# A two-layer recurrent block on one core: another order for the first batch's loads, up projections and attention chain

## What is computed

```python
xn = _layernorm(x, axis=-1)
s = _L0_attn_ref(xn, W_qkv, W_o)      # 16 heads of 16, ALiBi bias, causal softmax
g = _silu(_L0_ffn_ref(xn, W1, W2, W3))
x = x + s * g
xn = _layernorm(x, axis=-1)
s = _L1_attn_ref(...)                 # 16 heads of 128, RMS norm, rotation, soft cap, causal
g = _silu(_L1_ffn_ref(...))           # 16 routed experts, top 4, and a shared one
x = x + s * g
# inside _L0_ffn_ref, H = 1024:
hidden = jax.nn.silu(x @ W1.T) * (x @ W3.T)
out = fwht(hidden) @ W2.T             # Walsh-Hadamard transform along H
```

## Time and profile before

| | us |
|---|---|
| median of 3 runs | 1249.67 |
| lowest, highest | 1247.97, 1250.04 |
| the profiled execution, its own time | 1248.96 |
| its span | 1247.2 |

### The profile page before, as it was taken

How to read it: one execution, slowest core, us unless ns; L and a number is a source line. 1 busy time by engine, 2 the same in 40 slices (tenths; PEclk the granted TensorE clock), 3 DMA queues, 4 the chain that set the end, 5 groups by cost and what they waited for, 6 DMA issues and landing times.

```text
span 1247.2 us, 26623 instructions
## 1 busy us (share of the span) xinstructions
PE 1195.5 (96%) x9930; PEld 1048.9 (84%) x9930; DVE 845.9 (68%) x1691; ACT 601.9 (48%) x1353; POOL 498.9 (40%) x489
## 2 busy tenths in 40 slices
PE   4999999999988999999999999999999999999997
PEld 3788888888877777777789999999999999999996
DVE  3656777777677334434478888887887767777686
ACT  3444434444433455555545455554555455556443
POOL 0322334434444100000076776677664534454442
PEclk8999999999999999999999999999999999999999
DMA  6645335524739333333221111011010100000001
GB/s 205 249 162 178 109 115 204 190 74 162 241 133 374 95 107 103 105 106 103 79 91 38 50 33 60 26 65 31 26 60 1 35 1 1 1 1 1 1 27 43
DMA packets 65918, 114.93 MB, mean 92 GB/s; under 512 B 7937, under 2 KB 36481, under 8 KB 64385
## 3 DMA queue, kind: packets, MB, share of 16 engines
q1 hardware_dynamic: 59648, 96.45, 22.9%
q0 software_dynamic: 6144, 16.79, 4.1%
HBM read 48.85 MB, written 60.16 MB: 87 GB/s over the span
## 4 chain that ended last, share of the span: by engine, by line
PE 82%; DVE 6%; issue 5%; POOL 2%; ACT 2%; DMA 1%; SPq 1%; POOLq 0%; ACTq 0%; DVEq 0%
PE bank L837 8%; PE six L854 6%; PE bank L916 5%; PE bank L914 5%; PE bank L915 5%; PE six L955 5%; PE bank L992 2%; PE bank L990 2%; PE bank L991 2%; PE bank L927 2%; PE bank L926 2%; PE bank L928 2%; PE six L956 2%; PE bank L464 2%; PE six L979 2%
## 5 line engine op out<-in xcount | busy, mean ns | idle before, releaser
L1834 DVE TENSOR_TENSOR sq<-xs 128x512 f32<-128x512 f32 x128 | 131.1, 1024 | 39.3 <-ACT xs L1336 39.3
L2056 POOL TENSOR_TENSOR rstd<-msq,half_pow 128x8 f32<-128x8 f32 x64 | 105.9, 1655 | 96.0 <-DVE msq L1841 94.0
L1317 ACT ACTIVATE pT<-six,rstd 128x256 f32<-128x256 f32 x128 | 60.8, 475 | 169.0 <-PE six L956 169.0
L2068 POOL TENSOR_TENSOR pT<-pT,tri_mul 128x512 f32<-128x512 f32 x64 | 81.9, 1279 | 142.8 <-ACT pT L1365 142.8
L1981 POOL TENSOR_TENSOR hid_l<-hid,hid_h 128x256 fp32r<-128x256 f32 x64 | 50.4, 788 | 160.1 <-ACT hid_h L1092 160.0
L837 PE MATMUL bank<-experts,xT 128*128 x316 | 109.8, 470 | 0.8 <-ACT xT L1261 0.8
L914 PE MATMUL bank<-bw_h,xT1h 128*128 128x512 f32 x256 | 105.6, 413 | 0.8 <-ACT v L1341 0.8
L1405 DVE TENSOR_TENSOR yT1l<-six,yT1h 128x512 fp32r<-128x512 f32 x64 | 44.3, 692 | 84.7 <-ACT yT1h L1370 84.7
L916 PE MATMUL bank<-bw_l,xT1h 128*128 128x512 f32 x256 | 100.3, 392 | 0.0
L915 PE MATMUL bank<-bw_h,xT1l 128*128 128x512 f32 x256 | 99.9, 390 | 0.0
L2059 POOL TENSOR_TENSOR qn<-xs,rstd 128x256 f32<-128x256 f32 x128 | 91.4, 735 | 5.0
(11 more groups left out here) (315 smaller groups left out, 3820.8 us busy)
## 6 DMA issues: line engine op xcount, KB each, us to landing
cells_scratch<-zeros SPq DMA_DIRECT2D x8, 4352.0 KB, 16.5
xg<-cells_scratch SPq DMA_DIRECT2D x79, 128.0 KB, 2.0
cells_scratch<-y SPq DMA_DIRECT2D x79, 128.0 KB, 1.7
experts<-pack_experts_dram SPq DMA_DIRECT2D x16, 608.0 KB, 10.5
raw<-pack_attn_dram SPq DMA_DIRECT2D x8, 1024.0 KB, 5.0
qkA<-qkc SPq DMA_DIRECT2D x64, 64.0 KB, 2.4
w_full<-pack_w_dram SPq DMA_DIRECT2D x2, 1024.0 KB, 7.0
out_dram<-x_all SPq DMA_DIRECT2D x8, 256.0 KB, 2.1
```

Of the source, the lines that this page charges most:

```text
L1834: dve.tensor_tensor(out=sq[:, tt, :], in0=x_qk, in1=x_qk, op=ALU.mult).then_inc(sq_sb, 1)
L2056: pool.tensor_tensor(out=rstd[:, r, :], in0=msq[:, r, :], in1=half_pow[:], op=ALU.pow).then_inc(rstd_sb, 1)
```

## The change

Loads. w1 and w3 are loaded in halves: both first halves go ahead of stairs and k_rows, both second halves (`load_ffn(1)`) between the two spreads of the queries and keys. vo moves ahead of them all. The small constants, the gate bias and w2 move from behind the spreads to ahead of them. One semaphore for each half, `ffn_loaded[n]`, replaces `w1_loaded` and `w3_loaded`; the constants now count on `w2_loaded` with w2, so that POOL and `later_consts` wait for all five.

ACT and DVE, before the first batch: vo and the first half of w1 are converted ahead of `query_key`, the first half of w3 ahead of `values`. The second half of w1 is converted after the first `gate_tanh`, that of w3 after the first `heads_T`.

First batch. `up(0, 0)` and `up(0, 1)` come ahead of `scores(0, 0)`; `up(0, 2)` and `up(0, 3)` inside the first group's chain; the four `hadamard_mix` are placed one behind each of the blocks from `scores_T(0, 0)` to `mix(0, 1)`; `up(0, 4)` goes ahead of `scores(0, 3)`; `down(0, 4)` ahead of `scores(1, 0)`. ACT and DVE follow, with `later_consts` now ahead of the first `maxima`. What is computed stays the same, and so does the number of operations but for one load DMA in each of w1 and w3.

```diff
--- before.py
+++ after.py
...
@@ -313,10 +314,20 @@
             sp.dma_start(ident[:], ident_c).then_inc(ident_loaded, 16)
             sp.dma_start(q_row[:], q_row_c).then_inc(ident_loaded, 16)
             sp.dma_start(wqk_full[:].rearrange("p k c -> p (k c)"), pack_qk).then_inc(qk_loaded, 16)
+            sp.dma_start(wvo_full[:], pack_vo).then_inc(vo_loaded, 16)
+
+            def load_ffn(n):
+                for full, pack in ((w1_full, pack_w1), (w3_full, pack_w3)):
+                    sp.dma_start(ffn_half(full, n), ffn_half(pack.rearrange("p (k c) -> p k c", k=KD), n))\
+                      .then_inc(ffn_loaded[n], 16)
+
+            load_ffn(0)
             sp.dma_start(stairs32, stairs_c).then_inc(consts_loaded, 16)
             sp.dma_start(kA.rearrange("p g t -> p (g t)"), k_rows_c).then_inc(consts_loaded, 16)
-            sp.dma_start(wvo_full[:], pack_vo).then_inc(vo_loaded, 16)
-            sp.dma_start(w1_full[:].rearrange("p k c -> p (k c)"), pack_w1).then_inc(w1_loaded, 16)
+            for dst, src in ((hadamard, hadamard_c), (tri_mul, tri_mul_c), (before, before_c)):
+                sp.dma_start(dst[:], src).then_inc(w2_loaded, 16)
+            sp.dma_start(gate_bias[:], gate_b.partition_broadcast(P)).then_inc(w2_loaded, 16)
+            sp.dma_start(w2_a[:], pack_w2).then_inc(w2_loaded, 16)
 
             def spread(b, u):
 
@@ -330,12 +341,8 @@
             sp.wait_ge(consts_made, 1)
             sp.wait_ge(consts_loaded, 16 * N_CONST)
             spread(0, 0)
+            load_ffn(1)
             spread(0, 1)
-            for dst, src in ((hadamard, hadamard_c), (tri_mul, tri_mul_c), (before, before_c)):
-                sp.dma_start(dst[:], src).then_inc(w3_loaded, 16)
-            sp.dma_start(gate_bias[:], gate_b.partition_broadcast(P)).then_inc(w3_loaded, 16)
-            sp.dma_start(w3_full[:].rearrange("p k c -> p (k c)"), pack_w3).then_inc(w3_loaded, 16)
-            sp.dma_start(w2_a[:], pack_w2).then_inc(w2_loaded, 16)
             sp.dma_start(xs_all[:, TT:NT // 2, :],
                          x[1:NB // 2].rearrange("b (t p) d -> p (b t) d", p=P)).then_inc(x_loaded, 16)
             sp.dma_start(route_sb[:], route_c).then_inc(later_loaded, 16)
@@ -656,33 +663,37 @@
                 last.then_inc(fw_done, 1)
 
             def first_batch():
+                pe.wait_ge(wa_lo, 5)
+                pe.wait_ge(v0_sb, 1)
+                up(0, 0)
+                up(0, 1)
                 pe.wait_ge(consts_made, 2)
                 scores(0, 0)
+                pe.wait_ge(hid_sb, 1)
+                up(0, 2)
                 maxima_T(0, 0)
+                pe.wait_ge(hid_sb, 3)
+                up(0, 3)
                 scores_T(0, 0)
+                pe.wait_ge(hid_sb, 2)
+                pe.wait_ge(fw_lo, 1)
+                hadamard_mix(0)
                 scores(0, 1)
                 mix(0, 0, 0)
-                pe.wait_ge(wa_lo, 6)
-                up(0, 0)
+                hadamard_mix(1)
                 heads_back(0, 0)
                 maxima_T(0, 1)
-                up(0, 1)
                 scores_T(0, 1)
-                pe.wait_ge(hid_sb, 1)
-                up(0, 2)
+                hadamard_mix(2)
                 scores(0, 2)
                 mix(0, 1, 0)
-                pe.wait_ge(fw_lo, 1)
-                hadamard_mix(0)
-                pe.wait_ge(hid_sb, 2)
+                hadamard_mix(3)
                 heads_back(0, 1)
                 maxima_T(0, 2)
-                hadamard_mix(1)
                 scores_T(0, 2)
-                hadamard_mix(2)
-                hadamard_mix(3)
-                pe.wait_ge(hid_sb, 3)
-                up(0, 3)
+                pe.wait_ge(wa_lo, 7)
+                pe.wait_ge(hid_sb, 4)
+                up(0, 4)
                 pe.wait_ge(w2_lo, 4)
                 norm_T0(1)
                 down(0, 0)
@@ -692,25 +703,22 @@
                 project(1, 0)
                 heads_back(0, 2)
                 maxima_T(0, 3)
-                pe.wait_ge(hid_sb, 4)
-                pe.wait_ge(wa_lo, 7)
-                up(0, 4)
+                down(0, 1)
+                pe.wait_ge(hid_sb, 5)
+                up(0, 5)
                 scores_T(0, 3)
                 pe.wait_ge(qk_sb, 3)
                 project(1, 1)
-                down(0, 1)
-                pe.wait_ge(hid_sb, 5)
-                up(0, 5)
                 down(0, 2)
+                mix(0, 3, 0)
                 pe.wait_ge(qk_sb, 4)
                 up(0, 6)
-                mix(0, 3, 0)
+                heads_back(0, 3)
                 down(0, 3)
-                heads_back(0, 3)
                 pe.wait_ge(hid_sb, 6)
                 up(0, 7)
+                down(0, 4)
                 scores(1, 0)
-                down(0, 4)
                 down(0, 5)
 
             def batch(b, par, final):
@@ -1116,8 +1124,8 @@
                 o = bank[:, 0:TT * P].rearrange("p (t e) -> p t e", t=TT)
                 act.activation(r_th[:], o[:, :, 0:NE], ACT.Tanh, scale=0.5).then_inc(rth_sb, 1)
 
-            def ffn_hi(loaded, count, w, full, n):
-                act.wait_ge(loaded, 16 * count)
+            def ffn_hi(w, full, n):
+                act.wait_ge(ffn_loaded[n], 32)
                 act.activation(ffn_half(w, n), ffn_half(full, n), ACT.Copy).then_inc(wa_hi, 1)
 
             def hadamard_hi():
@@ -1137,37 +1145,37 @@
                                ACT.Copy).then_inc(v0_sb, 1)
 
             def first_batch():
-                ffn_hi(w3_loaded, N_W3, w3_h, w3_full, 0)
-                exps(0, 0)
-                ffn_hi(w3_loaded, N_W3, w3_h, w3_full, 1)
-                heads_T(0, 0)
                 gate_tanh(0, 0)
-                hadamard_hi()
                 gate_tanh(0, 1)
                 hidden_hi(0, 0)
-                exps(0, 1)
+                ffn_hi(w1_h, w1_full, 1)
                 hidden_hi(0, 1)
                 gate_tanh(0, 2)
+                hadamard_hi()
+                hidden_hi(0, 2)
+                gate_tanh(0, 3)
+                exps(0, 0)
+                hidden_hi(0, 3)
+                down_hi(0)
+                heads_T(0, 0)
+                ffn_hi(w3_h, w3_full, 1)
+                down_hi(1)
+                exps(0, 1)
+                down_hi(2)
                 heads_T(0, 1)
-                hidden_hi(0, 2)
-                down_hi(0)
+                down_hi(3)
                 exps(0, 2)
-                down_hi(1)
-                down_hi(2)
-                down_hi(3)
-                gate_tanh(0, 3)
+                gate_tanh(0, 4)
                 norm_T0(1)
-                hidden_hi(0, 3)
                 heads_T(0, 2)
                 query_key(1, 0)
-                gate_tanh(0, 4)
+                hidden_hi(0, 4)
+                gate_tanh(0, 5)
                 exps(0, 3)
                 query_key(1, 1)
-                hidden_hi(0, 4)
-                gate_tanh(0, 5)
+                hidden_hi(0, 5)
+                heads_T(0, 3)
                 gate_tanh(0, 6)
-                heads_T(0, 3)
-                hidden_hi(0, 5)
                 hidden_hi(0, 6)
                 gate_tanh(0, 7)
 
@@ -1218,12 +1226,12 @@
             qk_hi(0)
             qk_hi(1)
             norm_T0(0)
+            vo_hi()
+            ffn_hi(w1_h, w1_full, 0)
             query_key(0, 0)
             query_key(0, 1)
-            vo_hi()
+            ffn_hi(w3_h, w3_full, 0)
             values(0, 0)
-            ffn_hi(w1_loaded, 1, w1_h, w1_full, 0)
-            ffn_hi(w1_loaded, 1, w1_h, w1_full, 1)
             first_batch()
             for w in range(0, NB // 2 - 1):
...
@@ -1605,34 +1613,33 @@
                 dve.tensor_scalar(out=gate_bias[:], in0=gate_bias[:], scalar1=0.5, scalar2=None, op0=ALU.add)
 
             def first_batch():
+                hidden(0, 0)
+                hidden(0, 1)
+                later_consts()
                 maxima(0, 0)
+                hidden(0, 2)
                 queries_max(0, 0)
-                ffn_lo(5, w1_l, w1_full, w1_h, 1)
-                ffn_lo(6, w3_l, w3_full, w3_h, 0)
-                later_consts()
+                hadamard_lo()
+                hidden(0, 3)
+                ffn_lo(6, w1_l, w1_full, w1_h, 1)
+                down_lo(0)
                 maxima(0, 1)
+                heads_out(0, 0)
+                queries_max(0, 1)
+                stats(1, st0, mv0, ve0, st0_sb, mv0_sb, ve0_sb)
                 ffn_lo(7, w3_l, w3_full, w3_h, 1)
-                queries_max(0, 1)
-                hidden(0, 0)
-                heads_out(0, 0)
-                hadamard_lo()
-                hidden(0, 1)
-                hidden(0, 2)
-                maxima(0, 2)
-                queries_max(0, 2)
-                heads_out(0, 1)
-                stats(1, st0, mv0, ve0, st0_sb, mv0_sb, ve0_sb)
-                down_lo(0)
                 down_lo(1)
                 normalise(1, xn0[:, 1, :, :], mv0, rs0, rs0_sb, xn0_sb)
                 down_lo(2)
+                maxima(0, 2)
```

(23 more changed lines are left out.)

## The result

| | median us | runs | lowest, highest |
|---|---|---|---|
| before | 1249.17 | 7 | 1247.41, 1250.04 |
| changed | 1243.83 | 7 | 1242.80, 1246.90 |

The ratio is 0.9966, 95% interval 0.9956 to 0.9976: faster, by 3.0 to 5.5 us (the quotient of the two medians, 0.9957, is near the upper end of that gain). The profiled execution took 1243.83 us, its span is 1242.0 against 1247.2 us, 5.2 us less. I had forecast 8.8 us and 1240.2. The direction held, and the time lies in the wide range of 1237 to 1246. But it is outside the forecast's own range of 1238 to 1242, and the gain is only 0.6 of what the sum gave.

What follows compares the result with a forecast made beforehand. PE, 82% of the chain of waits, was taken to bound the kernel. Gains of 9.6 us less 0.8 at the batch's end gave 8.8, so 1248.96 became 1240.2; own range 1238 to 1242 (55%), eight in ten 1237 to 1246.

Steps and rivals of the forecast that it cites:

- What bounds the kernel, and what an early microsecond is worth: Whole execution: PE is 82% of the chain of waits; a microsecond saved early is one at the end while PE stays full.
- handed back at the end of the batch: Rival: batch 1's spread, cell clearing or loads hold to absolute times; remaining gain 2 to 3 us, 1246 to 1247; chance 5%.
- Start of `values`: Before the first batch: vo converted early, so values waits only for the second query_key and starts at 15.6 us.
- First up projection: Start of up(0,0): waits for w3's first half converted, w3_l from 17.9 to 19.1, so it starts at 19.1 us.
- The collision with POOL: DVE's w3_l waits behind POOL's first sum over w2, 15.5 to 17.9; up(0,0) starts at 19.1, without it 17.9.
- The second halves: Second-half loads of w1 and w3 in the first batch: landing 24.7 to 27.1 us, ACT's wait costing up to 3, taken as 0.
- queues in the way: Rival: POOL runs both sums first (2.3 us), second halves land late (up to 3), or both; 1242.5 to 1245.5; chance 12%.
- Low clock for longer: Rival: up(0,0), up(0,1) and the scores run at 1.2 GHz; price 2 to 4 us, 1242.2 to 1244.2; chance 22%.
- The clock: PE's clock in the first batch: high level before 18.3 us, no pause as long as 3.5 us, 1.00 from about 22.
- From the Hadamard part to `scores(0,3)`: First batch: 19.5 us of PE work and two DVE waits of 0.85 each; scores(0,3) starts at 49.6 against 57.6.
- The end of the batch: down(0,4) ahead of scores(1,0) no longer covers the maxima; PE's wait before norm_T0(2) grows 0.4 to 1.2, cost 0.8 us.
- Slower: Rival: clock stays low through the Hadamard part, 19 to 45 us; about 1254 us if it rises at 45; chance 4%.

Runs made afterwards that it cites:

- e5_consts_early: e1_act_order with the six later_consts operations on DVE made ahead of w3's first low half instead of the first maxima; 1238.92 us, ratio 0.9917.
- e4_fill: Changed kernel with 27 extra PE matmuls, results unused, in the pause ahead of up(0,3); 1241.23 us, ratio 0.9944.
- e1_act_order: Changed kernel with ACT's conversion of w1's second half moved from behind hidden_hi(0,0) to behind hidden_hi(0,2); 1240.63 us, ratio 0.9939.
- e8_down_behind: e5_consts_early with down(0,4) put back behind scores(1,0), as in the kernel before; 1238.31 us, ratio 0.9917.
- e3_x_behind: Changed kernel with SP waiting for the second halves to land before issuing x of batches 1 to 3 and later small loads; 1242.07 us, ratio 0.9950.

## Why the prediction was right or wrong

*What bounds the kernel, and what an early microsecond is worth*: right. The 5.2 us won at `norm_T0(2)` are the 5.2 us of the span. The rival that they are handed back at the end of the batch falls.

*Start of `values`*: right, 14.8 for 15.6; PE had been faster in `project`, because it rose inside it.

*First up projection*: 17.3 for 19.1. The collision with POOL that I priced at 1.2 us did not come: w2 landed at 17.3, not at 15.5, behind the end of `w3_l` at 16.95. It met the constants instead, where it cost 0.7 us. I had taken the wrong victim, since I did not ask it of each DVE operation in those 5 us. That `w3_l` got away is in part luck: in e5_consts_early it was issued 0.05 us ahead of POOL's first sum. So the 1.8 us here come from a collision that did not happen and from `values` being 0.8 us early, and they hid part of the miss that follows.

*The second halves*: this is the step that failed. "Up to 24.0 that costs nothing, at 24.7 up to 0.7, at 27.1 up to 3. I take 0, since only the 64 KB transfers are in the queue then." They landed at 26.2, 8.0 us from the second issue, and PE waited 3.3 us. My own bounds put that at some 2 us, and I chose the value that no row supported: the two rows that I had for such a load, 5.8 and 8.2 us, gave 24.7 and 27.1, both beyond the free limit. The reason that I gave, that only the spread's transfers are in the queue, was wrong too: x of the next batches and small loads were issued behind them from 21.5 us on, and with these held back the same load took 5.8 us. Even that would have been late. And the price was short in two ways. The limit of 24.0 was worked out for `up(0,0)` at 19.1; with 17.3 it would have been near 22.2 by the same sum, since a gain upstream makes a fixed landing later for those who wait for it. And the wait costs more than its length: the clock fell in PE's pause of 3.3 us, another 2 us (e4_fill). I had priced the low clock as a rival by itself, and late halves as another, without seeing that the second brings on the first. From the start of `up(0,0)` to the first Hadamard mix I had 11.0 us; the changed kernel needed 16.3, e1_act_order, without ACT's wait, 12.9, and e5_consts_early, without the constants too, 10.5. Of the rivals, "queues in the way" gave 1242.5 to 1245.5 for late halves or POOL, and came true by the halves alone. "Low clock for longer", 1242.2 to 1244.2, holds the measured time as well, but not by its own mechanism: `values` ran at the high level, and the low one came behind the wait.

*The clock*: half right. It was up when `values` ran, as I had concluded from the fall between 18 and 19 us. "The new order has no pause as long as that of 3.5 us" is true to the letter and no protection: 2.0 us, one pair of transposes, and 3.3 us were enough for a fall.

*From the Hadamard part to `scores(0,3)`*: 19.5 us for 19.5, both waits for DVE's queries 0.7 for 0.85. *The end of the batch*: the wait grew from 0.4 to 1.1 us, for 1.2, and e8_down_behind gets 0.7 of it back.

*Slower*: nothing of it. Even the loads alone are faster than before. Its 1254 us are not what its own rule gives: 25.9 us at half rate are 13.0 us of work, less the 1.7 of waits 11.3, and 1240.2 + 11.3 is about 1251.5.

The experiments add up: without ACT's wait 3.2 us, without the constants in front of the maxima another 1.7, and e5_consts_early stands at 1238.9, 1.3 us below the forecast.

## What to carry to other kernels

A conversion put in an engine's list is a promise that its load has landed: put it behind everything that others wait for, and price its wait by the rows for such a load, not by how empty the queue looks. When an edit moves work earlier, work out the slack of each fixed landing again with the new starting times, and take the clock into the price of every pause of PE. To learn what a pause costs beside its length, fill it with work that nobody uses, and compare from the start of the work behind it.

## What the runs showed of the hardware that I had not expected

Two loads of 512 KB with rows of 2 KB took from 5.8 to 8.0 us from the second issue to landing. Holding back x and the small loads behind them gave 5.8 twice, without that it was 6.9 to 8.0 in seven traces of eight; holding back the second spread as well changed nothing.

A clock that was up at 27 us fell inside `up(0,3)` in e1_act_order, with PE running again for 0.9 us behind waits of 2.1 and 0.3 us. In e3_x_behind the waits were 1.6 and 1.5 us, and it stayed up. So the sum of the waits alone did not tell which trace would fall.

DVE and POOL held each other up in both directions. In the changed kernel a 0.22 us cast took 0.56 and ended 0.1 us behind POOL's sum. In e5_consts_early DVE's `w3_l` was issued 0.05 us ahead of the two sums, took its usual 1.23 us, and POOL's sums took 5.76 instead of 4.73.

```profile
16.69 1.23 DVE L1413 TENSOR_TENSOR w_l<-w_full,w_h 128x1024 fp32r<-128x1024 f32 x1 [1.26 <-ACT w_h L1129]
...
16.74 5.76 POOL L1978 TENSOR_TENSOR x_all<-w_a 128x1024 f32<-128x1024 f32 x2 [10.56 <-DMA w_a<-pack_w_dram]
```
